# Attention and mixture-of-experts kernel on one core: order lists per engine in the attention stage

## What is computed

```python
h = group_norm(x, 32 groups) * gn_scale + gn_bias
q, k, v = Wq'h + bq, Wk'h + bk, Wv'h + bv                  # 128 x 1024 each
w = softmax(q'k * 128**-0.5, over keys)                    # 1024 x 1024
x = x + Wp'(v w') + bp
t = x as tokens                                            # 1024 x 128
t = t + linear_attention(layer_norm(t))                    # 4 heads of 32; softmax of k over tokens
u = layer_norm(t)
t = t + u + sum over the 2 best of 8 experts e of share_e * (gelu(u @ w1[e] + b1[e]) @ w2[e] + b2[e])
```

## Time and profile before

| | us |
|---|---|
| median of 3 executions | 338.52 (337.98 to 339.28) |
| the profiled execution's own time | 337.77 |
| its span, first to last instruction | 336.0 |
| TensorE busy in it | 303.2 |
| VectorE busy | 254.6 |
| ScalarE busy | 189.7 |
| GpSimd busy | 102.6 |
| mean granted TensorE clock | 0.989 |

### The profile page before, as it was taken

The page is one execution under the profiler, slowest core; times in us unless marked ns, Lnnn a source line. Parts: engine busy times, 40 slices in busy tenths (PEclk is TensorE's granted clock), DMA queues, the critical chain, the costliest instruction groups (busy, mean ns, idle before and its releaser), DMA issues.

```text
span 336.0 us, 5110 instructions
## 1 busy us (share of the span) xinstructions
PE 303.2 (90%) x1569; PEld 237.8 (71%) x1569; DVE 254.6 (76%) x591; ACT 189.7 (56%) x330; POOL 102.6 (31%) x154
## 2 busy tenths in 40 slices
PE   2798979979989889878988997999999997999996
PEld 2677758957878777666877785877767775666884
DVE  4999577577487598978689777787688685776995
ACT  1357464657560577346277666358567444856883
POOL 2464440059201754600446200089120037000000
PEclk9999999989999999999999999999999997999999
DMA  6702000010000011000000106386420692239501
GB/s 180 268 1 64 0 1 2 0 65 0 0 0 3 0 64 52 12 13 0 0 1 0 62 12 190 139 373 244 165 104 0 227 341 86 71 101 390 194 30 63
DMA packets 12757, 29.58 MB, mean 88 GB/s; under 512 B 2192, under 2 KB 5952, under 8 KB 10816
## 3 DMA queue, kind: packets, MB, share of 16 engines
q1 hardware_dynamic: 11872, 29.00, 24.5%
q10 hardware_dynamic: 864, 0.33, 0.4%
HBM read 24.73 MB, written 4.59 MB: 87 GB/s over the span
## 4 chain that ended last, share of the span: by engine, by line
PE 62%; DVE 23%; ACT 6%; issue 5%; POOL 2%; DMA 1%; DVEq 0%; POOLq 0%
PE ring L1379 7%; PE ring L1381 7%; PE ring L1380 7%; PE ring L1682 7%; PE ring L1394 7%; PE scores L1379 6%; PE scores L1381 6%; PE scores L1380 6%; DVE row_max L998 5%; DVE pT_lo L1004 4%; ACT prob L667 2%; PE ring L1531 2%; DVE lst L1034 2%; PE ring L1496 2%; ACT pT_hi L673 1%
## 5 line engine op out<-in xcount | busy, mean ns | idle before, releaser
L798 ACT ACTIVATE gel<-scores,b_c 128x512 f32<-128x512 f32 x64 | 43.9, 688 | 35.7 <-PE scores L1381 32.8
L1004 DVE TENSOR_TENSOR pT_lo<-ring,pT_hi 128x512 fp32r<-128x512 f32 x64 | 40.9, 680 | 15.3 <-ACT pT_hi L673 14.9
L998 DVE TENSOR_REDUCE row_max<-scores 128x1 f32<-128x1024 f32 x32 | 38.8, 1212 | 10.8 <-PE scores L1381 10.7
L667 ACT ACTIVATE prob<-scores,row_max 128x1024 f32<-128x1024 f32 x32 | 35.8, 1118 | 17.1 <-DVE row_max L998 17.0
L553 POOL TENSOR_SCALAR rstd<-lmv 128x8 f32<-128x8 f32 x8 | 2.1, 259 | 138.6 <-DVE lmv L1040 138.6
L673 ACT ACTIVATE pT_hi<-ring 128x512 fp32r<-128x512 f32 x64 | 35.0, 597 | 14.4 <-PE ring L1394 14.4
L1394 PE MATMUL ring<-ident,prob 128*128 128x128 f32 x256 | 35.3, 280 | 7.9 <-ACT prob L667 3.5
L1394 PEld LDWEIGHTS ring<-ident,prob 128*128 128x128 f32 x256 | 29.4, 143 | 12.9 <-ACT prob L667 4.5
L1379 PE MATMUL scores<-wT_hi,w_hi 128*128 128x512 f32 x64 | 34.4, 538 | 0.0
L1379 PE MATMUL scores<-k_both,q_hi 128*128 128x512 f32 x64 | 27.5, 429 | 1.0 <-DVE k_both L988 1.0
L1379 PE MATMUL ring<-pT_hi,v_hi 128*128 128x512 f32 x64 | 26.7, 417 | 1.2 <-DVE pT_lo L1004 1.2
(11 more groups left out here) (296 smaller groups left out, 721.0 us busy)
## 6 DMA issues: line engine op xcount, KB each, us to landing
pT_hi<-scratch_s SPq DMA_DIRECT2D x8, 1024.0 KB, 7.1
prob<-scratch_s SPq DMA_DIRECT2D x4, 1024.0 KB, 8.1
k_both<-scratch_s SPq DMA_DIRECT2D x3, 1024.0 KB, 5.7
z_in<-scratch_z SPq DMA_DIRECT2D x8, 256.0 KB, 2.9
out_dram<-out_s SPq DMA_DIRECT2D x8, 256.0 KB, 2.1
xb<-in_x_dram SPq DMA_DIRECT2D x3, 512.0 KB, 3.2
scratch_z<-out_s SPq DMA_DIRECT2D x2, 512.0 KB, 2.8
k_both<-scratch_s SPq DMA_DIRECT2D x4, 256.0 KB, 4.8
```

The lines of the kernel that those rows point to most:

```text
L667: act.activation(prob[:, i % 2, :], scores[:, 2 * (i % 2):2 * (i % 2) + 2, :].rearrange("p a t -> p (a t)"), ACT.Exp, bias=row_max[:, i:i ...
L798: act.activation(half(gel, s % 2), scores[:, s % 2, :], ACT.Gelu, bias=b1_c[:, s % E:s % E + 1]).then_inc(e_gelu, 1)
L998: dve.tensor_reduce(row_max[:, i:i + 1], scores[:, 2 * (i % 2):2 * (i % 2) + 2, :].rearrange("p a t -> p (a t)"), AX.X, ALU.max, negate=Tr ...
L1004: dve.tensor_tensor(tile_group(pT_lo, n, i), as_tiles(ps(place, unit)), tile_group(pT_hi, n, i).bitcast(FP32), ALU.subtract).then_inc(drai ...
```

## The change

The opening batch gets lists of its own; the other batches' lists are changed as follows, and the bank tables are written out as dictionaries for the new order.

- T5 goes right behind T4 on TensorE, ScalarE and VectorE, ahead of score 6, of p and c, of exp 6 and of row maximum 6. In the opening batch only ScalarE's list changes so (T5 ahead of exp 6); TensorE and VectorE keep T4, 6, T5, 7 there.
- In batches 1 to 3 ScalarE does exp 0, v, T0, exp 1, T1, exp 2; exp 1 stood ahead of v before.
- The high part of batch 0's x is made by ScalarE instead of VectorE, and VectorE's low parts go where the high parts were.
- The bias columns are issued by SP behind wk, ahead of wv, instead of by ACT.
- `first_norm` goes from ahead of the first projections on VectorE to behind the copy of wvT.
- Units p, c and T5 change banks in batches 1 to 3: T5a and T5b take the two banks behind T4b, then p0, p1, c0, c1.

Other edits only write loops and conditions out.

```diff
-def attention_units(linear, routing):
-        + ["gn_mean"] * (not L) + ROUTING["lg"] * R + T[3] + ["gn_var"] * (not L) + LINEAR["u"] * L
-        + ["lT"] * R + ROUTING["z"] * R + LINEAR["kT"] * L + ["PV0"] + T[4]
-        + LINEAR["p"] * L + ROUTING["c"] * R + T[5]
-        + ["g"] * L + ["OT0"]
+SECOND_UNITS = dict(T6a=0, T6b=1, q0=2, T7a=3, T7b=0, k0=1, k1=2, q1=3, PV1=0, OT1=0, v0=1, v1=2, T0a=3,
+                    T0b=0, T1a=1, T1b=2, xT0=3, xT1=0, T2a=1, T2b=2, T3a=3, T3b=0, u0=1, u1=2, kT0=3, kT1=0,
+                    PV0=1, T4a=2, T4b=3, T5a=0, T5b=1, p0=2, p1=3, g=0, OT0=1)
+LOOP_UNITS = dict(T6a=2, T6b=3, ctx=0, q0=1, T7a=2, T7b=3, m2=0, k0=1, k1=2, m3=3, q1=0, PV1=1, o0=2, o1=3,
+                  OT1=1, v0=0, v1=1, T0a=2, T0b=3, T1a=0, T1b=1, xT0=2, xT1=3, w0=0, w1=1, T2a=2, T2b=3,
+                  lg0=0, lg1=1, T3a=2, T3b=3, u0=0, u1=1, lT=2, z0=3, z1=0, kT0=1, kT1=2, PV0=3, T4a=0,
+                  T4b=1, T5a=2, T5b=3, p0=0, p1=1, c0=2, c1=3, g=0, OT0=1)
...
             sp.dma_start(wk_raw, wk).then_inc(ld_w["wk"], 16)
+            for i, v in enumerate((bq, bk, bv, bp)):
+                sp.dma_start(cols[:, i:i + 1], v.rearrange("(c a) -> c a", a=1)).then_inc(ld_w["cols"], 16)
...
             act.dma_start(wq_raw, wq).then_inc(ld_w["wq"], 16)
-            for i, v in enumerate((bq, bk, bv, bp)):
-                act.dma_start(cols[:, i:i + 1], v.rearrange("(c a) -> c a", a=1)).then_inc(ld_w["cols"], 16)
+            def split_first():
+                for n in range(HALVES):
+                    act.wait_ge(ld_x0b if n else ld_x[0], 16)
+                    act.activation(half(h_hi, n), half(xb, n), ACT.Copy).then_inc(h_hi_made, 1)
...
+            def opening_batch(place, after_place, b):
...
+                take_o(place, 0)
+                turn_probs(place, 4)
+                turn_probs(place, 5)
+                softmax(b, 6)
+                turn_probs(after_place, 6)
+                softmax(b, 7)
+            def batch(place, after_place, b, la, lc):
...
                 softmax(b, 0)
-                softmax(b, 1)
                 project_v(place)
                 turn_probs(place, 0)
+                softmax(b, 1)
                 turn_probs(place, 1)
                 softmax(b, 2)
...
                 take_o(place, 0)
                 turn_probs(place, 4)
-                if la is not None:
-                    turn_keys(place)
+                turn_probs(place, 5)
+                turn_keys(place)
                 softmax(b, 6)
-                turn_probs(place, 5)
                 turn_probs(after_place, 6)
                 softmax(b, 7)
...
             channel_means(0, 1)
-            high_first(0)
+            low_first(0)
             group_deviation(SETUP, 0, 1)
-            high_first(1)
+            low_first(1)
             group_variance(SETUP, 0, 1)
-            low_first(0)
-            low_first(1)
             first_weights()
-            first_norm()
...
+            def opening_batch(place, b):
...
+                take(place, "wvT", wvT[:, :])
+                first_norm()
+                group_stats(1)
+                row_maximum(b, 0)
...
                 turn_probs(place, b, 4)
+                turn_probs(place, b, 5)
                 row_maximum(b, 6)
                 if lc is not None:
                     turn_comb(place, lc, cT_early)
-                turn_probs(place, b, 5)
                 row_maximum(b, 7)
...
                 turn_probs(place, b, 4)
+                turn_probs(place, b, 5)
                 score(b, 6)
-                if la is not None:
-                    turn_keys(place)
+                turn_keys(place)
                 if lc is not None:
                     turn_comb(place, lc)
-                turn_probs(place, b, 5)
                 score(b, 7)
```

More of the change, by code:

```diff
@@ L49 @@
 ROUTING = dict(o=["o0", "o1"], w=["w0", "w1"], lg=["lg0", "lg1"], z=["z0", "z1"], c=["c0", "c1"])
-def attention_units(linear, routing):
[L55 to L62, removed]
-        + ["gn_mean"] * (not L) + ROUTING["lg"] * R + T[3] + ["gn_var"] * (not L) + LINEAR["u"] * L
-        + ["lT"] * R + ROUTING["z"] * R + LINEAR["kT"] * L + ["PV0"] + T[4]
-        + LINEAR["p"] * L + ROUTING["c"] * R + T[5]
-        + ["g"] * L + ["OT0"]
-    )
+FIRST_UNITS = dict(q0=3, k0=0, k1=1, q1=2, wvT=3, wpv=0, bias_o=1, v0=2, v1=3, T0a=0, T0b=1, l1qT=2,
+                   rowsT=3, T1a=0, T1b=1, xT0=2, xT1=3, T2a=0, T2b=1, gn_mean=2, T3a=3, T3b=0, gn_var=1,
+                   PV0=2, T4a=3, T4b=0, T5a=1, T5b=2, OT0=3)
+SECOND_UNITS = dict(T6a=0, T6b=1, q0=2, T7a=3, T7b=0, k0=1, k1=2, q1=3, PV1=0, OT1=0, v0=1, v1=2, T0a=3,
[5 more added lines that the diff above has]
+                  T4b=1, T5a=2, T5b=3, p0=0, p1=1, c0=2, c1=3, g=0, OT0=1)
+TAIL_FIRST = 2
 TAIL_UNITS = (ATTENTION["T"][6] + ["ctx"] + ATTENTION["T"][7] + ["m2", "m3", "PV1"] + ROUTING["o"]
@@ L110, in earlier, with placed @@
         return self.before[bank] + n
+def placed(banks, before):
+    count, found = list(before), {}
+    for unit, bank in banks.items():
+        found[unit] = (bank, count[bank] - before[bank])
+        count[bank] += 1
+    return Place(found, before), count
 def place_of(units, before, first=0, wide=None):
@@ L131, in conv_attention_moe @@
                        w_qkv, w_out, b_out, router, w1, b1, w2, b2, out):
[L133 to L138, removed]
+    SETUP, before = placed(SETUP_UNITS, [0] * 6)
+    FIRST, before = placed(FIRST_UNITS, before)
+    SECOND, before = placed(SECOND_UNITS, before)
+    LOOP, after_one = placed(LOOP_UNITS, before)
     loops = [n - k for n, k in zip(after_one, before)]
@@ L745, in batch @@
                 softmax(b, 2)
-                if la is not None:
-                    wait_drained(act, place, "OT1")
                 turn_x(place)
                 act.sem_inc(xb_read, 1)
[L751 to L767, removed]
+                turn_probs(place, 2)
@@ L1229, in batch @@
                     route_a()
-                if la is not None:
-                    key_maximum(place, la)
+                key_maximum(place, la)
                 if lc is not None:
@@ L1618, in batch @@
                 if lc is not None:
-                    for n in range(HALVES):
-                        turn_w(place, lc, n)
+                    turn_w(place, lc, 0)
+                    turn_w(place, lc, 1)
                 turn_probs(place, b, 2)
```

250 lines of the change are left out of this document (144 added, 106 removed).

## The result

| | before | after |
|---|---|---|
| median, first measurement (us) | 338.50 (337.98 to 339.28) | 334.72 (333.46 to 335.57) |
| ratio, 95% interval | | 0.9883 [0.9846, 0.9921] |
| the profiled execution's own time | 337.77 | 333.46 |
| its span | 336.0 | 331.3 |
| TensorE busy in it | 303.2 | 301.3 |

The forecast was 334.7 us. The median met it, but three of the terms behind it (the clock, the start, and T5 beside T4) did not hold as they were written, and one step of the change was misread. Two medians of this same kernel lie 0.8 us apart, so that the first one meets the forecast within 0.1 us is luck.

The account below looks back on a forecast made before the run. TensorE was taken to bound the kernel (VectorE's list up to 35 us), losing time in a handful of waits; 0.25 + 1.3 + 1.75 + 0.3 + 0.2 = 3.8 us off 338.52 gave 334.7 us, 8-in-10 range 333.2 to 336.7.

Parts of the forecast that it names:

- the clock: Batch 1, behind T2's wait: shorter waits keep TensorE at full clock, gaining about 1.1 us.
- the start: Before row maximum 0 of batch 0: shorter GpSimd step and later first_norm gain 0.25 us (bounds 0 and 1.0).
- T5 beside T4: Batches 1 to 3: q0 earlier, so following k0 starts 0.3 us (batch 1) and 0.2 us (batch 2) earlier; last batch 0.
- Opening batch, T5 ahead of exp 6: Batch 0: row maximum 7 and exp 7 come earlier, T7 starts at 48.85 us; gain 1.3 us.
- rival (b): Opening batch: T6b or q0 holds TensorE instead of exp 7, no gain there; 336.0 us, chance 0.12.
- Batch 1, exp 1 behind v: Batch 1: VectorE gets v earlier, T2 starts 0.65 us earlier despite a new T1 wait; nothing in batches 2 and 3.
- Rival (a): Batch 1: the clock falls all the same, so the 1.1 us go; 335.8 us, chance 0.14.
- rival (d): Batches 1 to 3: T1's added wait brings the clock down, up to 1.6 us each; 340.6 us, chance 0.06.
- Rival (e): Start: change doesn't do what it says, table load late or split waiting; loses some 0.5 us; 335.4 us, chance 0.06.
- Normalised h later: Start, VectorE: first_norm's pair moved behind wvT takes about 1.0 us instead of 2.01, leaving 1.2 us idle.
- Last T7 and experts: Last batch and expert stage: the 1.61 us wait before T7 stays, gain 0; experts only shift.

Follow-up runs that it names:

- e1: Kernel before with only the opening batch's new order (T5 ahead of exp 6 on ScalarE): 336.50 us, ratio 0.9923.
- e10: Changed kernel with exp 6 back ahead of T5 on ScalarE in the opening batch: 336.83 us, ratio 0.9934 to the kernel before.
- e2: Kernel before with only exp 1 moved behind v and T0 on ScalarE in batches 1 to 3: 337.67 us, ratio 0.9986.
- e5: Changed kernel with exp 1 back ahead of v in batches 1 to 3: 335.04 us, ratio 0.9913 to the kernel before.
- e3: Kernel before with only T5 right behind T4 on three engines in batches 1 to 3, with its banks: 338.55 us, ratio 0.9998.
- e4: Kernel before with only the new start (columns on SP, split on ScalarE, low parts earlier, second first_norm call): 338.09 us, ratio 0.9986.
- e6: Changed kernel without its first first_norm call, keeping only the one behind wvT: 333.70 us, ratio 0.9860 to the kernel before.
- e7: Changed kernel without its second first_norm call, keeping only the early one: 333.12 us, ratio 0.9854 to the kernel before.
- e11: Changed kernel with T5 back behind score 6, p, c and exp 6 in batches 1 to 3, with its banks: 335.38 us, ratio 0.9902.
- e9: The changed kernel measured again, unaltered, beside other kernels: 333.88 us, ratio 0.9878 to the kernel before.
- e12: Same kernel as e7 (changed kernel, only the early first_norm call), run once more: 332.83 us, ratio 0.9827 to the kernel before.
- e8: e7 with exp 7 also ahead of T6 on ScalarE in batches 1 to 3: 333.08 us, ratio 0.9848 to the kernel before.

## Why the prediction was right, and where it was not

**Opening batch, T5 ahead of exp 6: right.** Forecast 1.3 us, T7 at 48.85; measured 1.36 us and 48.78, with T5, row maximum 7, T6 and exp 7 in the order that the working gave, each within 0.3 us (row maximum 7 at 45.59 for 45.9, exp 7 at 47.52 for 47.6). e1 gives 1.20 and e10 1.12 us, so rival (b) is out. Its head start carries through batch 1.

**Batch 1, exp 1 behind v: the mechanism right.** Forecast 0.65 us and a wait of 0.7 at T1 and 0.8 at T2; measured 0.73, 0.49 and 0.64 (changed kernel and e2), and 0.72 when it is undone (e5). In batches 2 and 3 nothing, as forecast: v1 still waits 1.02 us and T1's wait of 0.57 us comes out of the one before w0, 1.28 before and 0.47 after.

**Batch 1's clock, 1.1 us: the size of that stretch right, the cause wrong.** From T2 to the turn of u took 6.27 us in the profile before and 5.22 after, 1.05 us, so the stretch costs what I said. But I took the wait of 2.09 us for its cause, on the strength of one profile. e1, e3 and e5 keep that wait and have full clock behind it (T2 to u 5.19, 5.21 and 5.20 us); e4, which has it too, has the fall. The profile before also held a second stretch, from 281.0 us on behind a wait of 1.86 us, which the working did not look at. The step that failed is "a gap of 2.09 us brings the clock down and one of 1.61 doesn't". What the runs show in its place: slow stretches of 3.4 us at the lower level, in places that differ from one program to the next. The profiles hold thirteen of them ahead of TensorE's last product. Each begins 0.1 to 2.1 us behind the end of a wait of TensorE of 1.0 to 2.1 us. So a wait seems to be needed, but a wait of a given length does not decide it. The wait of 1.84 to 1.88 us ahead of w_n in the experts is in all 14 profiles, and the clock falls behind it in four (before, e4, e5, e6); the wait of 2.09 us is in five, and it falls behind two. Here is the wait ahead of w_n in the kernel before, where the clock falls at 281.0, then in the changed kernel, where it stays up:

```profile
279.75 0.66 PE L1394 MATMUL scores<-ident,w_n 128*128 128x128 f32 x4 [1.86 <-POOL w_n L561]
```

```profile
275.60 0.66 PE L1412 MATMUL scores<-ident,w_n 128*128 128x128 f32 x4 [1.86 <-POOL w_n L564]
```

How many stretches an execution has depends on the kernel and on something that no run here shows. None of 54 executions of the kernel before had a mean clock above 0.995; 7 of 10 of the changed kernel had one of 0.998 or more. The mean clock rose from 0.9918 to 0.9973; since 3.4 us at half the clock lower the mean of such a span by 0.005, that is about 1.6 stretches per execution before and 0.5 after. By the 0.98 us per 0.005 above, 1.1 us of the change is clock (0.9 to 1.6 by the two other fits) and the remaining 3.0 us order: the mean times differ by 4.1 us (338.69 and 334.59). So the term of 1.1 us came out, but by luck: it stood for one stretch at one place, and what fell away is one stretch per execution at any place.

No single edit owns it: with the opening's order alone 3 of 7 executions have full clock, with exp 1 later alone 2 of 10, with T5 beside T4 or the new start alone none of 10. Undoing exp 1, the opening or T5 leaves 1 of 4, 5 of 12 and 1 of 7, against 7 of 10, which are too few to rank them. Rival (a) is right in saying that the clock may fall all the same, and wrong on where; rival (d) is out, since T1's new wait brought no fall in any batch of both profiles of the changed kernel. Its condition, though, that a wait of under 1.3 us could start the fall, is met in e2 (1.02 us, before 17.4 us), e3 (1.26) and e7 (1.11).

On this the Trainium skill ("TensorE: Matmul & The Clock Gate", section "HAM oscillation — how this bites in real kernels") has waits bring the clock down and the work behind them start slow. The thirteen stretches, each behind a wait (e10's behind T7's of 1.34 us), agree with it; e1, e3 and e5, full clock behind 2.1 us, do not bear it out as a rule for one gap.

**Start: forecast for an edit that was not made.** Forecast 0.25 us for the start with `first_norm` moved; e6, which moves it, gains 0.31 us against the landing of x (14.21 to 13.90). The change keeps the first call, so by the profiles its start loses 0.2 to 0.4 us instead (14.43 in e5 and e11, which have the same start, 14.49 and 14.61). By the executions of e4 at the same clock the new start gains 0.9 us, second call and all. What it is worth against the kernel before stays open between the two; what the second call costs does not, since e9 and e12 ran side by side. The split itself, the columns on SP and the shorter GpSimd step were read rightly; that step gave 0.37 us, and L525 behind it another 0.3 (0.57 for 0.90) that I had not priced. The remark that without the skill's rule the sum would be 0.1 us smaller was wrong by its own working: 18.2 us holds the 0.36 in full, and without it row maximum 0 would be no earlier than 18.42, so all of the 0.25 us would go. Rival (e) is half true: the change didn't do what I said, though the split isn't late. The step that failed is "Normalised h later": I took a line of context in the diff for a removed one.

**Heads of batches 2 and 3: close in the trace, not seen in the time.** Forecast 0.3 + 0.2, measured 0.39 + 0.34 in the changed kernel, 0.40 + 0.35 in e3, and T4 to T7 nearly unchanged (0.07 and 0.05). As forecast, q0 starts earlier and T7 is held by T6 and exp 7; score 7's delay does not reach it. At the same clock, however, e3 gains nothing over the kernel before (+0.3 us, 0.5 either way), nor e9 over e11. What the sum didn't have is the 0.4 us around the span. I know of no row that shows what it is: it is 2.05 to 2.23 us in e3, e5, e9 and e10, 1.76 to 2.13 in the kernels with one call of `first_norm` and T5 beside T4 (e6, e7, e8, e12), and 1.78 to 1.85 in e11, which lacks only that edit. It stays open.

**Last T7 and experts: right.** 1.61 us before and after; the experts' 0.44 us fits the second slow stretch of the profile before (280 to 286 us), not the edit: from the last T7 to the end e5, with such a stretch there, takes 130.62 us, and e9, without, 130.20.

In sum: order gives 1.36 + 0.20 + 0.73 + 0.39 + 0.34 + 0.19 (the small rest) = 3.2 us inside the span, less 0.4 around it: 2.8, near the 3.0 estimated above. Clock gives the other 1.1. This sum takes the start as the two profiles have it, level; if the new start is worth the 0.9 us that e4's executions say, some other term is smaller in the usual execution than in the profiles, and T5 beside T4 is the likely one (argued, not shown).

## What to carry to other kernels

Ask of each step on an engine's list what it delays on the engine next to it, and follow the delay until it meets a wait that is there anyway: that gave the distances in the trace within 0.2 us each here, save for the start. A distance in the trace is not yet time: compare executions at the same clock too, since one profile can be an unusual one. A slow stretch of the clock in one profile is no property of the instruction in front of it; before pricing it, look where other executions or variants of the kernel have theirs. And read a diff against the function as it stands: a call that remains beside its new copy cost 1 us, where all the reordering gave 3.

## What was not expected of the hardware

- The slow stretches: 3.4 us each at the lower level (a row of 0.72 over 6 us; the length from windows of 0.2 us), beginning at 72.8 and 281.0 us (before), 72.6 and 280.8 (e4), 144.8 (e1), 146.0 (e3), 17.4, 51.6 and 147.2 (e2), 277.2 (e5), 277.4 (e6), 142.2 (e7) and 50.8 (e10). e8, e11, e12 and both profiles of the changed kernel have none. Behind TensorE's last product the clock falls in every profile, with nothing left to slow down. A stretch costs 1.05 us in batch 1, 1.3 to 1.5 at the end of batch 2 (e1, e2, e3, e7), 1.4 and 1.6 at the head of batch 1 (e2, e10) and 0.4 in the experts (before). The place decides the price.
- TensorE's very first products can be slow while the granted clock reads 1.00. Their number belongs to the execution more than to the kernel: none or one in the profiles of the kernel before, e2, e4, e5, e6 and e11, two in e12, three and four in the two profiles of the changed kernel, four to six in e7, e10 and e8, eight in e1 and some ten in e3, at 0.43 us apart instead of 0.23:

```profile
11.57 0.48 PE L1379 MATMUL ring<-h_hi,wq_hi 128*128 128x512 f32 x1
11.89 0.40 PE L1380 MATMUL ring<-h_lo,wq_hi 128*128 128x512 f32 x1
```

```profile
10.84 0.77 PE L1397 MATMUL ring<-h_hi,wq_hi 128*128 128x512 f32 x1
11.41 0.63 PE L1398 MATMUL ring<-h_lo,wq_hi 128*128 128x512 f32 x1
```

  (the first two products of the kernel before, then of the changed one). In e1 row maximum 0 comes 0.95 us later for it than before and in e3 1.40 us, with nothing changed up to there. The changed kernel reaches these products 0.7 us earlier and starts the last of them only 0.1 us earlier; e5, with the same start and no more than one slow, starts the last 0.55 us earlier.
- GpSimd's steps on one column take 0.56 and 0.90 us beside VectorE's low parts and 0.19 and 0.57 us without them; VectorE's pair of line 924 takes 1.75 us while GpSimd clears buffers and 1.00 us when it waits.
